# Third routed layer: the experts of the first six batches chosen inside the third attention, those of the last two behind it

## The chip, the cores and the metric

The kernel runs on one core of a Trainium2 chip. The metric is the device time of one execution in microseconds; the median of three runs before the change is 1176.97 us (1175.15 to 1178.13). A core has five engines with queues of their own: TensorE (PE, matmuls), VectorE (DVE), ScalarE (ACT), GpSimd (POOL) and SyncE (SP, which issues most DMAs). Each works through its instructions in order and waits on semaphores.

## The reference

Eight batches of 128 tokens with 256 features go through four layers. Each layer adds a gated cross-attention to `x` and then a gated feed-forward part. The change is in layer 2 (the third), whose feed-forward part chooses two of 16 experts for each token:

```
affinity = sigmoid(x @ centroids.T)                    # per token, 16 values
_, top_idx = top_k(affinity + gate_bias, 2)            # lower index first among equals
top_aff = take_along_axis(affinity, top_idx)
weights = top_aff / (top_aff.sum(-1) + 1e-9)
out = 0.1 * swiglu(x, shared) + sum over the two of weights[k] * swiglu(x, expert[top_idx[k]])
```

Here `x` stands for the normalised tokens behind the layer's attention (16 heads, one unit for each batch).

## The kernel before

`plan()` writes one list of steps; each engine's program goes through that list and emits its part of every step. So the order of the list is the order of each engine's queue. Inside an attention the list is put together by `merge`, which sorts thunks by a key: a stream has a start and an end, and its thunks are spread evenly between. The keys are in units (one unit of the third attention is one batch), with offsets from `TIMES[2]` (L148): `body` 1.604, `span` 1.053, `start` 0.084, `end` 3.227.

For unit `u` of the third attention the body (`st`, `pv`, `onorm`, seven thunks) is spread from u+1.604 to u+2.657. In it `st` makes scores on PE that DVE clips (L2008) and ACT exponentiates (L1716); `pv` multiplies them with the values; `oev` copies the result (ACT, L1730); `onorm` transposes it (PE, L1460) and divides by the sum (DVE, L2019 and L2022), one for each of four groups of heads. Then come `ot` and `oy` (transposes L1469, output projection L1258, DVE L2040 to L2045) and `oz` with `stats` (second normalisation and statistics of `x`, DVE L2055 to L2058 and L1877 to L1879, POOL L2409 and L2356). Behind each unit the finished batch is normalised (`fn`, DVE L1812), stored for the gathers (`tokens`, SP L1092), transposed (`xt`, L1266) and multiplied with the centroids (`xl`, PE L1258, copied to `lg` at L2063), at keys between u+3.327 and u+4.127. So the logits of batch 5 are there while unit 7 is in its body.

Behind the attention `sorted_pairs()` (L622) begins with a barrier on the last statistics. Then: `iota`; the shared expert's first two products `gu(0, 0)` and `gu(0, 1)` on PE (L1624, 16 matmul records); `route`, in which DVE chooses both experts of all eight batches (L2159 to L2186) with one exponential on ACT (L1744), and releases PE's count matmuls (L1501 to L1505) through `route_pe`; silu (ACT, L1797) and product (`gated2`, DVE, L2296) of the first half; `gu(1, 0)` and `gu(1, 1)`; `rank2`, in which DVE turns the counts into slots (from L2189); `invert` (PE L1611, DVE L2305 to L2311), which gives the token list; the loads of sorted tokens by POOL (L2429); `down2` (PE L1635, DVE L2321); then 31 tiles of sorted tokens (`tx`, `tu`, `th`, `td`), between which SP loads the keys of the next attention (`k3load`). Each of DVE's instructions in `route` and `rank2` waits for the one before it (`link`).

`first_max` (L1851) is the search for the first largest of the scores, five instructions; `route` uses it twice. The buffers `ra`, `rb`, `rc`, `oh` and `cm` lie in the third slot of `Pt`, where the attention's exponentials also go (columns 0 to 511 of each slot in this attention).

Of the kernel before, what the change touches and what calls it, by code (L numbers as in the profile page):

```python
# [72 lines left out]
P = 128  # L73
NB = 8
# [10 lines left out]
LOADS = 14  # L85
FFN1 = (11.35, 13.3, -0.95, 1.5, -0.9, 1.4)
FIRST_GROUP = 6
KEY_SPACE = 4
QUANT_PIECES = 5
SLOTW = 6144  # L90
# [62 lines left out]
def plan():  # L153
# [6 lines left out]
    def take(ring):  # L160
        ring = "B" if ring in "MS" else ring
        n[ring] += 1
        if ring == "B":
            s_count[(n["B"] - 1) % BANKS] = (n["B"] - 1) // BANKS + 1
        return n[ring] - 1

    def add(kind, **k):
        s = Record(kind=kind, **k)
        steps.append(s)
        return s  # L170
# [83 lines left out]
    def attention(A, later, before):  # L254
# [196 lines left out]
        for u in range(A.U):  # L451
            first, store, packs = front(u)
            if "fronts" in at:
                times = at["rest"] if u and "rest" in at else at["fronts"]
                assert len(times) == len(first)
                streams += [([thunk], u + t, u + t) for thunk, t in zip(first, times)]
            else:
                streams += [(first, u, u + at["front"])]
            streams += [(store, u + at["store"], u + at["store"]),
                        (packs, u + at["packs"], u + at["packs"] + 0.02)]  # L460
            if A.layer == 0:
                streams += [([lambda r=units[u]: add("bias", un=r)], u + at["body"], u + at["body"])]
            if A.layer == 0 and u == 0:
                at_group = FIRST_GROUP - 1 + at["end"]
                streams += [([lambda: choose0(0)], at_group + 0.95, at_group + 0.95),
                            ([lambda: rank0(0)], at_group + 1.3, at_group + 1.3),
                            ([lambda b=b: add("scatter", b=b) for b in range(FIRST_GROUP)], at_group + 1.45, at_group + 1.6)]
                streams += [([lambda: add("prepare", m=take("M"))], at["front"], at["front"]),
                            ([lambda: add("bias_out", m=take("M"))], at["max_first"], at["max_first"]),
                            ([lambda i=i: add("loads", i=i) for i in range(LOADS)], 2.0, 9.5)]  # L470
            if A.layer == 3 and u == 1:
                streams += [([lambda: add("w12load", s=last["td"])], u + at["body"] + 0.5, u + at["body"] + 0.5)]
            if A.has_max:
                begin = u + at["max"] if u else at["max_first"]
                step = (u + at["max_end"] - begin) / A.parts
                for tiles, split, turn in maxes(units[u]):
                    begin += step
                    streams += [(tiles, begin - step, begin), ([split], begin, begin),
                                ([turn], begin + at["neg"] - at["max_end"], begin + at["neg"] - at["max_end"])]
            body_end = u + at["body"] + at["span"]  # L480
            batches = range(units[u].b0, units[u].b0 + A.nb)
            streams += [(body(units[u]), u + at["body"], body_end), (finish(units[u]), body_end + at["start"], u + at["end"]),
                        ([f for b in batches for f in later(b)], u + at["end"] + 0.1, u + at["end"] + 0.9)]
# [26 lines left out]

    def group0(g):
        return (0, FIRST_GROUP) if g == 0 else (FIRST_GROUP, NB)

    def choose0(g):
        add("choose0", lm=last["lm"], exp_i=take("exp"), j=g, k=group0(g))
# [106 lines left out]
    def sorted_pairs():  # L622
# [5 lines left out]
        add("iota", m=take("M"))  # L628
        for ch in range(2):
            gate_up2(0, ch)()  # L630
        m_route = take("M")
        route(2, m_route)
        for tg in range(2):
            for ch in range(2):
                if tg:
# [115 lines left out]
def flamingo(nc, t, out):  # L751
# [13 lines left out]
    with ExitStack() as ctx:  # L765
# [53 lines left out]
        def expert(e, word, n):  # L819
# [59 lines left out]

        ra, rb, rc, oh, cm = [Pt[:, 2, 128 * i:128 * (i + 1)].rearrange("p (b e) -> p b e", b=NB)
                              for i in range(5)]
        ra0, rc0, oh0 = [tmp2[:, 64 * i:64 * (i + 1)].rearrange("p (b e) -> p b e", b=NB) for i in range(3)]
        sg = Pt[:, 0:2, 0:512]
        xe = qf[:, :, 0:256]
# [361 lines left out]
        def _(pe):  # L1248
# [36 lines left out]
            for s in steps:  # L1285
# [204 lines left out]
                elif s.kind == "rank0":  # L1490
# [4 lines left out]
                    pe.matmul(dst, lhsT=const("before"), rhs=oh0[:, b0:b1, :], start=True, stop=False)  # L1495
                    pe.matmul(dst, lhsT=const("ones"), rhs=rc0[:, b0:b1, :], start=False, stop=True
                              ).then_inc(bank_ready[s.m % BANKS], 1)
                elif s.kind == "route" and s.layer == 2:
                    dst = m_begin(s.m)
                    pe.wait_ge(route_pe, 1)  # L1500
                    pe.matmul(dst[:, 0:128], lhsT=const("before"), rhs=cm[:, :, :], start=True, stop=False)  # L1501
# [139 lines left out]
        def _(act):  # L1641
# [4 lines left out]
            for s in steps:  # L1646
# [90 lines left out]
                elif s.kind == "choose0":  # L1737
                    b0, b1 = s.k
                    act.wait_ge(route_a, s.exp_i + 1)
                    act.activation(ra0[:, b0:b1, :], ra0[:, b0:b1, :], ACT.Exp).then_inc(route_b, 1)  # L1740
                elif s.kind == "route":
                    act.wait_ge(route_a, s.exp_i + 1)
                    n = {2: 16, 3: 4}[s.layer]
                    act.activation(ra[:, :, 0:n], ra[:, :, 0:n], ACT.Exp, scale=-1.0 if s.layer == 2 else 1.0  # L1744
                                   ).then_inc(route_b, 1)
                elif s.kind == "ext":
                    e = s.i
                    turn(act, bank_ready, s.m)
# [52 lines left out]
        def _(dve):  # L1801
# [46 lines left out]
                link(dve.tensor_reduce(tmp2[:, 0:n // 4], tmp[:, 0:n].rearrange("p (w t) -> p w t", t=4), AX.X, ALU.add))  # L1848
                link(dve.tensor_copy(te[:, 0:n // 4], tmp2[:, 0:n // 4]))

            def first_max(src, E, onehot):  # L1851

                link(dve.tensor_reduce(r8[:, 0, :], src, AX.X, ALU.max))
                mx = r8[:, 0, :].unsqueeze(2).to_broadcast([P, NB, E])
                link(dve.tensor_tensor(rb[:, :, 0:E], src, mx, ALU.is_equal))
                desc = const("desc")[:, 0:E].unsqueeze(1).to_broadcast([P, NB, E])
                link(dve.tensor_tensor(rb[:, :, 0:E], rb[:, :, 0:E], desc, ALU.mult))
                link(dve.tensor_reduce(r8[:, 1, :], rb[:, :, 0:E], AX.X, ALU.max))
                m2 = r8[:, 1, :].unsqueeze(2).to_broadcast([P, NB, E])
                link(dve.tensor_tensor(onehot, rb[:, :, 0:E], m2, ALU.is_equal))  # L1860

            dve.memset(arena[:, 0:2048], 0.0)
            dve.memset(arena[:, 6144:8192], 0.0).then_inc(zeroed[0], 1)
# [4 lines left out]
            for s in steps:  # L1868
# [241 lines left out]
                    link(dve.tensor_tensor(gate, gate, keep, ALU.mult))  # L2110
                elif s.kind == "route":
                    evacuated(dve, s.lm)
                    n = {2: 16, 3: 4}[s.layer]
                    L = lg[:, :, 0:n]
                    if s.layer == 3:
                        link(dve.tensor_tensor(L, L, row("br3").unsqueeze(1).to_broadcast([P, NB, n]), ALU.add))
                    if s.layer == 3:
                        first_max(L, n, oh[:, :, 0:n])
                        mx = r8[:, 0, :].unsqueeze(2).to_broadcast([P, NB, n])
                        dve.tensor_tensor(ra[:, :, 0:n], L, mx, ALU.subtract).then_inc(route_a, 1)  # L2120
                        dve.wait_ge(route_b, s.exp_i + 1)
# [4 lines left out]
                    if s.layer == 3:  # L2126
# [27 lines left out]
                        link(dve.tensor_scalar(r8[:, 5, :], r8[:, 5, :], float(P), None, ALU.mult))  # L2154
                        link(dve.tensor_tensor(r8[:, 5, :], r8[:, 5, :], r8[:, 4, :], ALU.add))
                        dve.tensor_copy(idx[:, 0, :], r8[:, 5, :]).then_inc(routed3, 1)
                    else:

                        link(dve.tensor_scalar(ra[:, :, :], L, -87.0, None, ALU.max))  # L2159
                        dve.sem_inc(route_a, 1)  # L2160
                        dve.wait_ge(route_b, s.exp_i + 1)
                        link(dve.tensor_scalar(rc[:, :, :], ra[:, :, :], 1.0, None, ALU.add))
                        link(dve.reciprocal(ra[:, :, :], rc[:, :, :]))
                        gb = row("gb2").unsqueeze(1).to_broadcast([P, NB, 16])
                        link(dve.tensor_tensor(rc[:, :, :], ra[:, :, :], gb, ALU.add))
                        first_max(rc[:, :, :], 16, oh[:, :, :])
                        link(dve.tensor_scalar(lg[:, :, :], oh[:, :, :], -1e30, None, ALU.mult))
                        link(dve.tensor_tensor(rc[:, :, :], rc[:, :, :], lg[:, :, :], ALU.add))
                        first_max(rc[:, :, :], 16, lg[:, :, :])

                        for k, pick in enumerate((oh, lg)):
                            link(dve.tensor_tensor(cm[:, :, :], pick[:, :, :], ra[:, :, :], ALU.mult))
                            link(dve.tensor_reduce(wts[:, k, :], cm[:, :, :], AX.X, ALU.add))
                        link(dve.tensor_tensor(r8[:, 2, :], wts[:, 0, :], wts[:, 1, :], ALU.add))
                        link(dve.tensor_scalar(r8[:, 2, :], r8[:, 2, :], 1e-9, None, ALU.add))
                        link(dve.reciprocal(r8[:, 3, :], r8[:, 2, :]))
                        link(dve.tensor_scalar(r8[:, 3, :], r8[:, 3, :], tg[:, 6:7], None, ALU.mult))
                        link(dve.tensor_tensor(wts[:, :, :], wts[:, :, :], r8[:, 3, :].unsqueeze(1).to_broadcast([P, 2, NB]),
                                               ALU.mult))

                        link(dve.tensor_tensor(cm[:, :, :], oh[:, :, :], lg[:, :, :], ALU.add))
                        link(dve.memset(rc[:, 0, :], 0.0))
                        for b in range(1, NB):
                            link(dve.tensor_tensor(rc[:, b, :], rc[:, b - 1, :], cm[:, b - 1, :], ALU.add))
                        link(dve.tensor_tensor(ra[:, 0, :], rc[:, NB - 1, :], cm[:, NB - 1, :], ALU.add))
                        dve.sem_inc(route_pe, 1)  # L2186
                elif s.kind == "rank2":
# [367 lines left out]
```

## Time and profile before

| | us |
|---|---|
| median of three runs | 1176.97 |
| their range | 1175.15 to 1178.13 |
| the profiled execution | 1181.53 |
| its span, first to last instruction | 1179.7 |
| PE busy | 946.2 |
| DVE busy | 666.4 |
| ACT busy | 437.7 |
| POOL busy | 396.5 |

Busy time is the sum over all stages. An engine that is busy 80% of the span need not set its end: what counts at a place is which wait there ends last. The chain of waits follows the instruction that ended last back to what released it, step by step. A row of a timeline that says `[2.02 <-DVEq L2186]` tells that the engine sat idle for 2.02 us and that DVE's queue at line 2186 released it. The granted clock (PEclk) is a share of TensorE's full speed of 2.4 GHz.

### The profile page before, as it was taken

The numbers are of one execution on the slowest core, as the hardware profiler recorded it, in microseconds if no ns is written. First come the engines' busy times: TensorE is split into PE (matmuls) and PEld (weight loads), VectorE is DVE, ScalarE is ACT, GpSimd is POOL, SyncE is SP. The second block draws the span as 40 slices with busy tenths as digits, with TensorE's granted clock in tenths as the row PEclk, the third lists the DMA queues.
The fourth block names the chain that finished last, engine by engine and source line by source line (L and its number), as shares of the span: only waits on it lengthen the run. The fifth ranks groups of instructions, "written<-read, shape, count | busy, mean of one in ns | idle before, by whom it ended". The sixth has DMA issues, their size and how long they took to land.

```text
span 1179.7 us, 18929 instructions
## 1 busy us (share of the span) xinstructions
PE 946.2 (80%) x6638; PEld 557.1 (47%) x6638; DVE 666.4 (56%) x1588; ACT 437.7 (37%) x722; POOL 396.5 (34%) x530
## 2 busy tenths in 40 slices
PE   3899995789189999787699627999989997199992
PEld 1455544678044455565367412344434444156652
DVE  5778753452679433687663258788887852211111
ACT  1356662111046412444114200566556575022120
POOL 5232304332622003343034261356555565200002
PEclk9999997989579999898699956799999999599997
DMA  6434424684633003744318630101210002700002
GB/s 183 123 94 156 154 104 179 195 256 160 152 99 103 1 1 73 221 97 94 152 54 233 151 102 5 38 2 42 109 42 3 2 2 108 269 20 23 14 14 80
DMA packets 110107, 115.27 MB, mean 98 GB/s; under 512 B 58696, under 2 KB 99336, under 8 KB 106984
## 3 DMA queue, kind: packets, MB, share of 16 engines
q1 hardware_dynamic: 102912, 97.67, 26.9%
q0 software_dynamic: 3792, 10.36, 3.6%
q10 hardware_dynamic: 3312, 6.03, 1.4%
q8 instruction: 56, 0.92, 0.3%
q14 instruction: 35, 0.29, 0.1%
HBM read 88.17 MB, written 29.62 MB: 100 GB/s over the span
## 4 chain that ended last, share of the span: by engine, by line
PE 47%; DVE 15%; DMA 8%; issue 6%; POOL 4%; ACT 2%; SPq 1%; POOLq 0%; ACTq 0%; DVEq 0%
PE psT L1558 7%; PE psT L1258 6%; PE psT L1409 5%; PE psB L1373 4%; PE psB L1258 4%; DVE mxp L1972 4%; PE psO L1453 4%; PE psB L1572 3%; PE psB L1635 2%; DMA xn<-scr_tokens,token 2%; PE psO L1443 2%; PE psT L1521 2%; PE psO L1441 1%; PE psB L1599 1%; DMA scr_k_high<-sk 1%
## 5 line engine op out<-in xcount | busy, mean ns | idle before, releaser
L1972 DVE TENSOR_REDUCE mxp<-psB 128x1 f32<-128x512 f32 x256 | 163.7, 683 | 37.6 <-PE psB L1373 36.8
L1409 PE MATMUL psT<-whole 99*128 99x256 bf16 (+2 forms) x1024 | 153.3, 275 | 10.8 <-issue 10.0
L1976 DVE TENSOR_REDUCE mxp<-psB 128x2 f32<-128x512 f32 x192 | 123.4, 683 | 32.1 <-PE psB L1379 31.8
L1722 ACT ACTIVATE Pt<-psT,ln 128x1024 f32<-128x1024 f32 x96 | 106.5, 1113 | 64.6 <-PE psT L1409 63.5
L1409 PEld LDWEIGHTS psT<-whole 99*128 99x128 bf16 (+2 forms) x1024 | 96.6, 102 | 55.1 <-issue 22.9
L1722 ACT ACTIVATE Pt<-psT 128x1024 f32<-128x1024 f32 x96 | 97.9, 1023 | 57.6 <-PE psT L1409 56.1
L1373 PE MATMUL psB<-whole 96*128 96x512 bf16 x256 | 96.3, 427 | 24.6 <-DMA whole<-scr_q 14.0
L2356 POOL TENSOR_TENSOR rstd<-vare,cst 128x1 f32<-128x1 f32 x64 | 35.8, 562 | 231.0 <-DVE vare L1879 230.7
L1379 PE MATMUL psB<-whole 96*128 96x256 bf16 x384 | 78.2, 306 | 37.8 <-DMA whole<-scr_q 20.9
L1558 PE MATMUL psT<-whole,qf 128*128 x176 | 80.7, 602 | 0.6 <-ACT qf L1770 0.6
L2415 POOL TENSOR_SCALAR nb_t<-Pt 128x1024 f16<-128x1024 f32 x64 | 67.2, 1050 | 40.1 <-ACT Pt L1722 38.0
L1379 PEld LDWEIGHTS psB<-whole 96*128 96x128 bf16 x384 | 30.4, 104 | 86.3 <-issue 36.3
L2268 DVE TENSOR_TENSOR Pt<-psT,Pt 128x512 f32<-128x512 f32 x22 | 15.2, 691 | 98.7 <-ACT Pt L1776 98.7
L1441 PE MATMUL psO<-Pt,whole 128*32 128x256 f32 x768 | 63.2, 402 | 3.9 <-ACT Pt L1722 3.0
L1373 PEld LDWEIGHTS psB<-whole 96*128 96x128 bf16 x256 | 20.6, 100 | 89.0 <-issue 39.5
L1258 PE MATMUL psT<-xn_t,whole 128*128 128x512 f32 (+1 forms) x128 | 61.4, 631 | 0.0
L1453 PE MATMUL psO<-Pt,cst 128*32 128x256 f32 x768 | 59.0, 384 | 0.0
L2449 POOL DMA_INDIRECT xn_t<-scr_sorted_out,idx x8 | 7.6, 953 | 138.9 <-DMA scr_sorted_out<-xn 136.7
L1266 PE MATMUL psB<-cst,xn 128*128 128x128 f32 x96 | 22.9, 326 | 32.5 <-DVE xn L1812 31.7
L1460 PE MATMUL psB<-cst,Oe 128*128 128x128 f32 x160 | 37.6, 303 | 13.5 <-ACT Oe L1730 8.4
L1558 PEld LDWEIGHTS psT<-whole,qf 128*128 128x128 f32 x176 | 32.4, 194 | 33.4 <-issue 33.4
L2429 POOL DMA_INDIRECT xn<-scr_tokens,token x31 | 29.4, 949 | 53.8 <-DVE token L2311 28.6
(340 smaller groups left out, 1758.4 us busy)
## 6 DMA issues: line engine op xcount, KB each, us to landing
whole<-in_w SPq DMA_DIRECT2D x32, 512.0 KB, 5.3
whole<-in_w SPq DMA_DIRECT2D x5, 3072.0 KB, 10.7
scr_q<-sq SPq DMA_DIRECT2D x48, 96.0 KB, 2.1
whole<-scr_q SPq DMA_DIRECT2D x24, 192.0 KB
whole<-scr_k SPq DMA_DIRECT2D x24, 192.0 KB, 5.5
scr_sorted_out<-xn SPq DMA_DIRECT2D x31, 128.0 KB, 4.4
scr_k<-sk SPq DMA_DIRECT2D x32, 96.0 KB, 1.9
whole<-scr_k SPq DMA_DIRECT2D x24, 128.0 KB, 5.6
```

The source lines that it names most:

```text
L1258: ins = pe.matmul(dst, lhsT=lhs(kd), rhs=rhs(kd), start=(kd == 0), stop=(kd == halves - 1))
L1373: ins = pe.matmul(dst, lhsT=q_at[:, h * A.T + s.tc * P:h * A.T + (s.tc + 1) * P], rhs=k_at[:, h * NT + half * 512:h * NT + (half + 1) * 51 ...
L1379: ins = pe.matmul(dst[:, i * 256:(i + 1) * 256], lhsT=q_at[:, h * A.T + s.tc * P:h * A.T + (s.tc + 1) * P], rhs=k_at[:, h * A.T:(h + 1) * ...
L1409: ins = pe.matmul(psT[:, s.n % 2, i * A.T:(i + 1) * A.T], lhsT=k_at[:, h * kw + s.c * P:h * kw + (s.c + 1) * P], rhs=q_at[:, h * A.T:(h + ...
L1441: ins = pe.matmul(dst, lhsT=VA[:, u.g % 3, s.c * A.H + h, :], rhs=pr, start=first, stop=last)
L1453: ins = pe.matmul(dst, lhsT=const("sumsel"), rhs=pr, start=False, stop=last)
L1460: ins = pe.transpose(dst[:, tc * P:(tc + 1) * P], Oe[:, s.o % 2, tc * P:(tc + 1) * P], ident)
L1558: ins = pe.matmul(psT[:, s.n % 2, k * 512:(k + 1) * 512], lhsT=xeT[:, s.i % 2, kd, :], rhs=whole[:, bass.ds(s.un.k * SLOTW + at, 512)], st ...
L1722: act.activation(p_slot(A, s.p)[:, 0:4 * A.T], psT[:, s.n % 2, 0:4 * A.T], ACT.Exp, bias=bias, scale=scale).then_inc(T_used[s.n % 2], 1)
L1972: dve.tensor_reduce(mxp[:, s.un.g % 2, at:at + 1], psB[:, s.n % BANKS, :], AX.X, ALU.max).then_inc(bank_used[s.n % BANKS], 1)
L1976: dve.tensor_reduce(mxp[:, s.un.g % 2, at:at + 2], psB[:, s.n % BANKS, :].rearrange("p (h n) -> p h n", h=2), AX.X, ALU.max).then_inc(bank ...
L2415: pool.tensor_scalar(n_slot(s.p)[:, 0:w], p_slot(s.A, s.p)[:, 0:w], 1.0, OFFSET, ALU.mult, ALU.add).then_inc(rounded, 1)
```

## The change

The routing of layer 2 is cut into two groups of batches, 0 to 5 and 6 to 7. Each group has two steps: `scores2` (bound the logits on DVE, exponential on ACT) and `choose2` (all the rest of the choice on DVE, on the group's columns alone). The running count over the batches carries on from the first group to the second, whose `choose2` makes the total and releases the counts, a step of its own (`counts2`) with the same matmuls. The first group's steps are put into the third attention with the keys `at_group + 0.95` and `at_group + 1.2`, where `at_group` is 5 + 3.227; the second group's stand where `route` stood. The buffers move to columns 512 to 1023 of the third slot of `Pt`, and `cm` to the second slot, so that the attention's exponentials don't meet them. Layer 3 keeps `route`, with the same instructions.

```diff
+CHOOSE2_AT = 1.2
+SECOND_GROUP = 6
...
+            if A.layer == 2 and u == 0:
+                at_group = SECOND_GROUP - 1 + at["end"]
+                streams += [([lambda: scores2(0)], at_group + 0.95, at_group + 0.95),
+                            ([lambda: choose2(0)], at_group + CHOOSE2_AT, at_group + CHOOSE2_AT)]
...
+    def group2(g):
+        return (0, SECOND_GROUP) if g == 0 else (SECOND_GROUP, NB)
+
+    def scores2(g):
+        last["exp2"] = add("scores2", lm=last["lm"], exp_i=take("exp"), k=group2(g)).exp_i
+
+    def choose2(g):
+        add("choose2", exp_i=last["exp2"], k=group2(g))
...
             gate_up2(0, ch)()
-        m_route = take("M")
-        route(2, m_route)
+        scores2(1)
+        choose2(1)
+        m_route = add("counts2", m=take("M")).m
...
-        ra, rb, rc, oh, cm = [Pt[:, 2, 128 * i:128 * (i + 1)].rearrange("p (b e) -> p b e", b=NB)
-                              for i in range(5)]
+        ra, rb, rc, oh = [Pt[:, 2, 512 + 128 * i:640 + 128 * i].rearrange("p (b e) -> p b e", b=NB) for i in range(4)]
+        cm = Pt[:, 1, 768:896].rearrange("p (b e) -> p b e", b=NB)
...
-                elif s.kind == "route" and s.layer == 2:
+                elif s.kind == "counts2":
...
+                elif s.kind == "scores2":
+                    b0, b1 = s.k
+                    act.wait_ge(route_a, s.exp_i + 1)
+                    act.activation(ra[:, b0:b1, :], ra[:, b0:b1, :], ACT.Exp, scale=-1.0).then_inc(route_b, 1)
...
-            def first_max(src, E, onehot):
...
+            def first_max(src, E, onehot, b0, b1):
+                def wide(ap):
+                    return ap.unsqueeze(2).to_broadcast([P, b1 - b0, E])
+                work = rb[:, b0:b1, 0:E]
+                link(dve.tensor_reduce(r8[:, 0, b0:b1], src, AX.X, ALU.max))
+                link(dve.tensor_tensor(work, src, wide(r8[:, 0, b0:b1]), ALU.is_equal))
+                desc = const("desc")[:, 0:E].unsqueeze(1).to_broadcast([P, b1 - b0, E])
+                link(dve.tensor_tensor(work, work, desc, ALU.mult))
+                link(dve.tensor_reduce(r8[:, 1, b0:b1], work, AX.X, ALU.max))
+                link(dve.tensor_tensor(onehot, work, wide(r8[:, 1, b0:b1]), ALU.is_equal))
...
+                elif s.kind == "scores2":
+                    evacuated(dve, s.lm)
+                    b0, b1 = s.k
+                    dve.tensor_scalar(ra[:, b0:b1, :], lg[:, b0:b1, :], -87.0, None, ALU.max).then_inc(route_a, 1)
+                elif s.kind == "choose2":
+                    b0, b1 = s.k
+                    score, biased, first, second, both = [t[:, b0:b1, :] for t in (ra, rc, oh, lg, cm)]
+                    total, scale = r8[:, 2, b0:b1], r8[:, 3, b0:b1]
+                    dve.wait_ge(route_b, s.exp_i + 1)
+                    link(dve.tensor_scalar(biased, score, 1.0, None, ALU.add))
+                    link(dve.reciprocal(score, biased))
+                    gb = row("gb2").unsqueeze(1).to_broadcast([P, b1 - b0, 16])
+                    link(dve.tensor_tensor(biased, score, gb, ALU.add))
+                    first_max(biased, 16, first, b0, b1)
+                    link(dve.tensor_scalar(second, first, -1e30, None, ALU.mult))
+                    link(dve.tensor_tensor(biased, biased, second, ALU.add))
+                    first_max(biased, 16, second, b0, b1)
+
+                    for k, pick in enumerate((first, second)):
+                        link(dve.tensor_tensor(both, pick, score, ALU.mult))
+                        link(dve.tensor_reduce(wts[:, k, b0:b1], both, AX.X, ALU.add))
+                    link(dve.tensor_tensor(total, wts[:, 0, b0:b1], wts[:, 1, b0:b1], ALU.add))
+                    link(dve.tensor_scalar(total, total, 1e-9, None, ALU.add))
+                    link(dve.reciprocal(scale, total))
+                    link(dve.tensor_scalar(scale, scale, tg[:, 6:7], None, ALU.mult))
+                    link(dve.tensor_tensor(wts[:, :, b0:b1], wts[:, :, b0:b1],
+                                           scale.unsqueeze(1).to_broadcast([P, 2, b1 - b0]), ALU.mult))
+
+                    link(dve.tensor_tensor(both, first, second, ALU.add))
+                    if b0 == 0:
                         link(dve.memset(rc[:, 0, :], 0.0))
-                        for b in range(1, NB):
-                            link(dve.tensor_tensor(rc[:, b, :], rc[:, b - 1, :], cm[:, b - 1, :], ALU.add))
+                    for b in range(max(b0, 1), b1):
+                        link(dve.tensor_tensor(rc[:, b, :], rc[:, b - 1, :], cm[:, b - 1, :], ALU.add))
+                    if b1 == NB:
                         link(dve.tensor_tensor(ra[:, 0, :], rc[:, NB - 1, :], cm[:, NB - 1, :], ALU.add))
                         dve.sem_inc(route_pe, 1)
...
```

## Rows read from the trace of the kernel before

**Rows 1.** The page's head: the span of the profiled execution.
```profile
span 1179.7 us, 18929 instructions
```

**Rows 2.** Chain of waits, three stretches: start us, us, what was waited for.
```profile
565.91 0.66 PE psB L1266 x2
...
567.56 2.06 PE psB L1258 x4
569.64 0.43 DVE y_t L2040
...
579.39 0.24 DVE Pt L2159
...
620.39 8.03 DMA xn<-scr_tokens,token
...
1036.82 3.44 PE psT L1558 x8
```

**Rows 3.** Timeline of DVE, 560 to 570: start us, us, instruction, [idle before, releaser].
```profile
561.47 0.18 DVE L2019 RECIPROCAL rden<-psB 128x4 f32<-128x4 f32 x1 [0.21 <-DVE nb_t L2008]
...
564.67 0.22 DVE L2022 TENSOR_TENSOR On<-psB,rden 128x64 f32<-128x64 f32 x1
565.00 0.18 DVE L2019 RECIPROCAL rden<-psB 128x4 f32<-128x4 f32 x1
...
565.89 0.23 DVE L2022 TENSOR_TENSOR On<-psB,rden 128x64 f32<-128x64 f32 x1
569.64 0.42 DVE L2040 TENSOR_TENSOR y_t<-psB,rows 128x256 f32<-128x256 f32 x1 [3.53 <-PE psB L1258]
```

**Rows 4.** The same timeline of DVE, 579 to 602.
```profile
579.39 0.23 DVE L2159 TENSOR_SCALAR Pt<-lg 128x128 f32<-128x128 f32 x1
580.12 0.23 DVE L2162 TENSOR_SCALAR Pt<-Pt 128x128 f32<-128x128 f32 x1 [0.49 <-ACT Pt L1744]
580.38 0.95 DVE L2163 RECIPROCAL Pt<-Pt 128x128 f32<-128x128 f32 x1
581.37 0.29 DVE L2165 TENSOR_TENSOR Pt<-Pt,rows 128x128 f32<-128x128 f32 x1
...
587.22 0.20 DVE L2176 RECIPROCAL r<-r 128x8 f32<-128x8 f32 x1
...
588.40 1.43 DVE L2184 TENSOR_TENSOR Pt<-Pt 128x16 f32<-128x16 f32 x7
...
591.39 0.28 DVE L2189 COPY Pt<-psB 128x128 f32<-128x128 f32 x1
...
601.53 0.19 DVE L1847 TENSOR_TENSOR tmp<-tmp,w_at 128x32 f32<-128x32 f32 x1
```

**Rows 5.** Timeline of PE, 578 to 610.
```profile
578.56 9.67 PE L1258 MATMUL psT<-xn_t,whole 128*128 128x512 f32 x16
590.24 0.46 PE L1501 MATMUL psB<-Pt,cst 128*128 128x128 f32 x2 [2.02 <-DVEq L2186]
...
591.11 8.59 PE L1258 MATMUL psT<-xn_t,whole 128*128 128x512 f32 x16
599.98 0.63 PE L1611 MATMUL psB<-whole 128*128 128x64 bf16 x16 [0.28 <-DVE whole L2225]
...
604.77 4.58 PE L1635 MATMUL psB<-whole 128*128 128x256 f32 x20 [0.67 <-DVE x L2321]
```

**Rows 6.** Timeline of ACT, the silu behind the second `gu`.
```profile
588.27 0.60 ACT L1797 ACTIVATE nb_t<-psT 128x512 f32<-128x512 f32 x1 [2.84 <-PE psT L1258]
```

**Rows 7.** Stretches of the span; columns PE, PEld, DVE, ACT, POOL busy, PEclk, DMA share, GB/s.
```profile
564.00:566.00 2.00, 0.46 (x2) 0.20 (x3) 1.73 (x10) 0.00 (x0) 0.55 (x1) 0.50 0.00 0
...
582.00:584.00 2.00, 2.00 (x4) 0.93 (x3) 1.78 (x7) 0.00 (x0) 0.00 (x0) 0.54 0.96 406
...
590.00:595.00 5.00, 4.76 (x12) 2.76 (x13) 4.48 (x15) 0.00 (x0) 0.00 (x0) 0.66 0.00 0
...
605.00:610.00 5.00, 4.79 (x24) 3.99 (x23) 2.92 (x7) 0.39 (x2) 2.99 (x4) 1.00 0.35 105
```

More of the change, by code:

```diff
@@ L1740, in _ @@
                     act.activation(ra0[:, b0:b1, :], ra0[:, b0:b1, :], ACT.Exp).then_inc(route_b, 1)
+                elif s.kind == "scores2":
+                    b0, b1 = s.k
+                    act.wait_ge(route_a, s.exp_i + 1)
+                    act.activation(ra[:, b0:b1, :], ra[:, b0:b1, :], ACT.Exp, scale=-1.0).then_inc(route_b, 1)
                 elif s.kind == "route":
                     act.wait_ge(route_a, s.exp_i + 1)
-                    n = {2: 16, 3: 4}[s.layer]
-                    act.activation(ra[:, :, 0:n], ra[:, :, 0:n], ACT.Exp, scale=-1.0 if s.layer == 2 else 1.0
-                                   ).then_inc(route_b, 1)
+                    act.activation(ra[:, :, 0:4], ra[:, :, 0:4], ACT.Exp).then_inc(route_b, 1)
                 elif s.kind == "ext":
@@ L1849, in pack_tiles @@
                 link(dve.tensor_copy(te[:, 0:n // 4], tmp2[:, 0:n // 4]))
-            def first_max(src, E, onehot):
[L1853 to L1860, printed above, removed]
+            def first_max(src, E, onehot, b0, b1):
[8 more added lines that the diff above has]
+                link(dve.tensor_tensor(onehot, work, wide(r8[:, 1, b0:b1]), ALU.is_equal))
             dve.memset(arena[:, 0:2048], 0.0)
@@ L2112, in _ @@
                     evacuated(dve, s.lm)
-                    n = {2: 16, 3: 4}[s.layer]
+                    n = 4
                     L = lg[:, :, 0:n]
@@ L2117, in _ @@
                     if s.layer == 3:
-                        first_max(L, n, oh[:, :, 0:n])
+                        first_max(L, n, oh[:, :, 0:n], 0, NB)
                         mx = r8[:, 0, :].unsqueeze(2).to_broadcast([P, NB, n])
@@ L2156, in _ @@
                         dve.tensor_copy(idx[:, 0, :], r8[:, 5, :]).then_inc(routed3, 1)
[L2157 to L2181, printed above, removed]
```

## The prediction

> **What bounds the kernel now.** I read four views, in this order. The page first: one execution of 1179.7 us span [rows 1], a serial mix of engines. Then the chain of waits around the change. It runs without a break through the last unit of the third attention and the head of the third routed layer: DVE's last normalisations and `xn`, PE's transpose and output projection, DVE's `y_t`, and so on to the routing block at 579.39 [rows 2]. Each link waits for the one before, so a microsecond put on DVE's queue in front of one of them is a microsecond of the kernel, unless it falls into one of DVE's idle gaps. So the third view is DVE's timeline. From 561.47 to 566.12 DVE goes from one instruction to the next (only the first row shows an idle time, 0.21 us before it); its first real gap, 3.53 us, comes after the last `onorm` of the attention and before `y_t` at 569.64 [rows 3]. The routing block then holds DVE from 579.39 and ends with the eighth addition of the running count near 590.04 (seven of them 588.40 to 589.83, one more 0.2 behind): 10.65 us [rows 4]. The fourth view is PE beside it: the two shared-expert steps `gu(0, 0)` and `gu(0, 1)` take it from 578.56 to 588.23, then it idles 2.02 us, until the routing block has released the count matmuls at 590.24 [rows 5]. So PE is only 2.0 us better than DVE here. Call T the start of the routing block: DVE releases the counts at T+10.65, PE could take them at T+8.84.
>
> **What the change does to the queues.** No step of PE changes place. On DVE one block becomes two. The place of the first follows from the planner's keys. Unit 7's `body` has seven thunks between 8.604 and 9.657, so its sixth, with `pv(3)` and `onorm(2)`, has the key 9.431; the block `choose2(0)` gets 5+3.227+1.2 = 9.427 and stands just in front of it. `scores2(0)` (9.177) stands behind `oz(6)` and its `stats`, before `onorm(1)`. On DVE that is: one instruction before 564.67, and the whole choice of six batches between the end of `onorm(1)` and 565.00 [rows 3]. Behind it wait `onorm(2)`, `fn(6)`, `onorm(3)`, all that follows from them on PE, ACT and POOL, and the token stores on SP's queue. The 3.53 us gap lies behind the block, not under it.
>
> **Cost of the first block (six batches, 96 columns instead of 128).** An instruction costs its duration and about 0.03 us to the next (580.12+0.23 to 580.38; 580.38+0.95 to 581.37). A fp32 one with a tensor operand takes 0.29 at 128 columns [rows 4], the 32-column one 0.19 (the row at 601.53 of [rows 4]), so 0.255 at 96, with the gap 0.29. There are 17 of these (the biased score, five and five in the two searches for a maximum, the masked copy, four for the weights, the sum of both picks): 4.9 us. Two `tensor_scalar` of 0.23 at most, 0.25 each: 0.5. The reciprocal: 0.95 at 128 columns, 0.20 at 8, so 0.75 at 96, with its gap 0.8. Five small ones, of which the reciprocal at 587.22 is one, at 0.23: 1.1. The memset 0.1. The running count goes from seven additions to five, at 1.43/7 = 0.20: 1.0. Sum 8.4, with a doubt of 0.2 either way. `scores2(0)` adds 0.2 before `onorm(1)`. The exponential between them is hidden: DVE to ACT and back took 580.12-579.39 = 0.73 [rows 4], 0.5 of it after DVE's own instruction, and `onorm(1)` fills just that (its two instructions stand from 564.46 to 565.00 in the same view; the second is in [rows 3]). ACT holds behind `scores2(0)` the last two copies of the attention's output, but what they feed stands behind the block on DVE anyway. I take **8.6 us**. Ends: 7.7 if ACT and PE work that used to trail DVE is then ready and closes small gaps (the idle 0.21 and a part of the 0.66 of transposes), 9.3 if the exponential is waited for in full. It cannot go under the 3.53 gap, since the gap begins only when PE has what stands behind the block; were it placed there, the price would be 8.6-3.5 = 5.1.
>
> **What the second block saves (two batches, 32 columns).** Seventeen at 0.22 = 3.75; two at 0.21 = 0.4; reciprocal 0.20 + (0.75/120)*24 = 0.35, with the gap 0.4; five small 1.1; two additions and the last one 0.6; the score step 0.65 (0.73 with a narrower pair). Sum 6.9, against 10.65: DVE releases the counts 3.7 us earlier. But PE isn't there yet: `gu(0, 1)` ends at T+8.84 as before. The work of DVE was what covered those matmuls; with it gone, they are late next. The counts can start at T+8.87 instead of T+10.85, 1.97 earlier. Then `rank2` needs DVE, which first has the second `gated2`: its silu starts at T+8.88 [rows 6], ends 0.60 later, the product takes 0.6, so `rank2` starts at about T+10.15 against 591.39-579.39 = 12.0 [rows 4]. Gain **1.85 us**. From there DVE runs `rank2` to the release of `invert` in the same time. PE's `gu(1, 0)` and `gu(1, 1)` took 8.59 beside it, ending 0.28 before `invert` [rows 5]; they start 1.9 earlier too. Everything behind (`invert`, the token list, POOL's loads, `down2`) moves as one piece. Bounds of the gain: 3.7 if PE is out of the way (eight records of this shape take 3.44 us at full clock [rows 2], so the 16 need 6.9 and end at T+6.1), and -2.1 if the clock stays at half throughout (13.8, ending at T+12.9).
>
> **The clock.** TensorE was granted half its clock (1.2 GHz) in the attention's tail, the stretch 564 to 566 standing for all two-us stretches from 560 to 582; it rose to full (2.4 GHz) at the end of 582 to 584, some 5 us into `gu(0, 0)` [rows 7]. Then, after the 2.02 us in which PE idled for the counts, the stretch 590 to 595 reads 0.66. In the changed kernel that first gap closes, so `gu(1, 0)` may run at full clock; DVE's `rank2` is then the bound and nothing is won, while a gap of about 2 us opens in front of `invert` instead. The earlier gap of this size was followed by half clock, but a third of the five us from 590 to 595 was at full again, so I take the slowed stretch behind the new gap to be over before DVE frees the bank for the fourth `down2` product: 20 records that then ran at full in 4.58 us [rows 5, 7]. At worst these run at half and cost 4.6 more. The Trainium skill (TensorE: Matmul & The Clock Gate, "HAM oscillation — how this bites in real kernels") says that idle stretches between bursts of matmuls put the clock back to half, and that each burst then starts slow. The trace agrees with it at 590. If the rule struck `down2` whole, the sum would be near +11; by the rows it is +6.75.
>
> **Sum.** 8.6 - 1.85 = +6.75 us on the profiled execution (1181.53 us, of which the span is 1179.7). That execution lies 4.6 above the median of the runs, 1176.97, and none of the stretches is one that varies; so 1176.97+6.75 = **1183.7 us**, 0.57% slower. Below 0.3% (3.5 us) a measurement of this kernel, whose three runs spread over 3 us, can't tell a change from none.
>
> **Rivals.**
> (a) DVE alone bounds the head of the layer: the clock rises early enough that `gu(0, 1)` is done before the second block. Gain 3.7: +4.9, 1181.9. For it: the rise came 5 us into PE's work and may come earlier. Against: a whole 2 us must be found.
> (b) The clock goes the other way: late in `gu(0, 0)` (+2.1 in place of -1.85), or half through `down2` (+4.6). +10.7 or +11.4, taken as 1187.7. For it: the row at 0.66 after a gap of the same size. Against: DVE covers the first part of `down2`.
> (c) The first block falls into PE's wait after all (a late `onorm` on DVE costs nothing because the transposes were not ready): 5.1-1.85 = +3.3, 1180.2, within the bound. Against: no idle before 566.12 on DVE.
> (d) Not slower: the 31 tiles behind the routing wait three times about 8 us (the first 8.03 [rows 2]) for an indirect load of tokens, while the key loads for the next attention share the DMA engines. If the new phase between PE, POOL and SP lets one of these loads land ahead of the key load, a wait goes: 6.75-8.0 = -1.3, 1175.7; two of them, 1168. It decides from a load that is issued one key load earlier. Against: both streams are released by the same tile steps and move together.
>
> **Chances.** Forecast 0.60, (a) 0.10, (b) 0.12, (c) 0.09, (d) 0.09. Slower by over 0.3%: forecast, (a) and (b), 0.82. Within 0.3%: (c) and half of (d), 0.14. Faster: 0.04. The range from 1179.5 to 1188.5 holds the forecast with its 7.7 to 9.3 for the block, (a), (b) and (c), and leaves out (d).
>
> **What the changed profile would show.** Right: some 34 DVE instructions in one piece between `onorm(1)` and `onorm(2)` of the last unit, 8.4 us, in the chain of waits, with PE and ACT idle beside the end of it; then the same 3.53 us gap; from `scores2(1)` to the counts 8.9 us, with the count matmuls waiting for no engine and standing directly behind `gu(0, 1)`; the clock at full in `gu(1, 0)`. Wrong: the 3.53 gap shorter or gone (c), a DVE wait before the counts (a), `gu(0, 0)` at half through its end or `down2` over 8 us (b), fewer than three waits of about 8 us in the tiles (d). A time under 1180.5 would refute the forecast.

## The result, and the profile after

The changed kernel takes 1181.65 us (median of 20 runs, 1174.93 to 1184.97), the kernel before 1176.77 us on the same occasions (20 runs, 1171.67 to 1184.7). The ratio is 1.0035 with a 95% interval of 1.002 to 1.0051: +4.1 us (2.4 to 6.0), slower, as forecast. Timed differences here and below come from the ratio, applied to the time of the kernel before; the two medians alone differ by 4.9 us. The forecast was +6.75 us, which lies outside the interval.

The profiled execution has a span of 1178.3 us, 1.4 less than that of before, though the kernel is slower. So spans don't show where the time went; stretches do. DVE's timeline of the attention's last unit comes first (start, duration, instruction, and in brackets the idle time before it with its releaser):

```profile
560.28 0.20 DVE L2178 TENSOR_SCALAR Pt<-lg 128x96 f32<-128x96 f32 x1
560.39 0.17 DVE L2037 RECIPROCAL rden<-psB 128x4 f32<-128x4 f32 x1
560.60 0.22 DVE L2040 TENSOR_TENSOR On<-psB,rden 128x64 f32<-128x64 f32 x1
560.83 0.22 DVE L2184 TENSOR_SCALAR Pt<-Pt 128x96 f32<-128x96 f32 x1
561.08 0.75 DVE L2185 RECIPROCAL Pt<-Pt 128x96 f32<-128x96 f32 x1
561.87 0.26 DVE L2187 TENSOR_TENSOR Pt<-Pt,rows 128x96 f32<-128x96 f32 x1
...
568.30 1.01 DVE L2207 TENSOR_TENSOR Pt<-Pt 128x16 f32<-128x16 f32 x5
569.34 0.18 DVE L2037 RECIPROCAL rden<-psB 128x4 f32<-128x4 f32 x1
...
573.99 0.42 DVE L2058 TENSOR_TENSOR y_t<-psB,rows 128x256 f32<-128x256 f32 x1 [3.54 <-PE psB L1274]
```

The first block stands between `onorm(1)` and `onorm(2)`, from 560.83 to 569.34: 8.51 us without an idle time, and behind it the same gap as before, 3.54 in place of 3.53 [rows 3]. The second block, behind the barrier, in the same view:

```profile
583.74 0.18 DVE L2178 TENSOR_SCALAR Pt<-lg 128x32 f32<-128x32 f32 x1
584.28 0.18 DVE L2184 TENSOR_SCALAR Pt<-Pt 128x32 f32<-128x32 f32 x1 [0.35 <-ACT Pt L1760]
584.50 0.35 DVE L2185 RECIPROCAL Pt<-Pt 128x32 f32<-128x32 f32 x1
584.88 0.19 DVE L2187 TENSOR_TENSOR Pt<-Pt,rows 128x32 f32<-128x32 f32 x1
...
590.38 0.17 DVE L2209 TENSOR_TENSOR Pt<-Pt 128x16 f32<-128x16 f32 x1
590.70 0.69 DVE L2320 TENSOR_TENSOR whole<-psT,nb_t 128x512 f32<-128x512 f32 x1
592.04 0.69 DVE L2320 TENSOR_TENSOR whole<-psT,nb_t 128x512 f32<-128x512 f32 x1 [0.65 <-ACT nb_t L1815]
592.65 0.28 DVE L2213 COPY Pt<-psB 128x128 f32<-128x128 f32 x1
```

T is now 583.74. DVE releases the counts at T+6.8 (against T+10.65), then has to wait 0.65 us for the silu of `gu(0, 1)`, and `rank2` starts at T+8.91 in place of T+12.0 [rows 4]. PE's timeline beside it:

```profile
582.91 8.46 PE L1274 MATMUL psT<-xn_t,whole 128*128 128x512 f32 x16
591.21 0.38 PE L1517 MATMUL psB<-Pt,cst 128*128 128x128 f32 x2
...
591.80 7.11 PE L1274 MATMUL psT<-xn_t,whole 128*128 128x512 f32 x16
601.24 0.63 PE L1627 MATMUL psB<-whole 128*128 128x64 bf16 x16 [2.33 <-DVE whole L2249]
```

The count matmuls follow `gu(0, 1)` with no idle time where 2.02 us stood before [rows 5]; `gu(1, 0)` and `gu(1, 1)` take 7.11 in place of 8.59; a gap of 2.33 us has opened before `invert`. The clock (sixth value behind the stretch's length: PE, PEld, DVE, ACT, POOL busy, PEclk, DMA share, GB/s):

```profile
582.00:584.00 2.00, 2.00 (x7) 1.48 (x7) 0.80 (x4) 0.00 (x0) 0.00 (x0) 0.50 0.59 221
584.00:586.00 2.00, 2.00 (x3) 0.78 (x3) 1.48 (x7) 1.51 (x2) 0.00 (x0) 0.55 0.94 406
586.00:588.00 2.00, 2.00 (x6) 0.95 (x5) 1.70 (x9) 0.02 (x1) 0.00 (x0) 1.00 1.16 487
...
600.00:605.00 5.00, 3.21 (x28) 2.59 (x28) 4.51 (x15) 0.00 (x0) 0.00 (x0) 1.00 0.00 0
```

It rose some 3 us into `gu(0, 0)`, in the profile of before 5 us into it [rows 7], and it stayed at full through the new gap.

All the stretches side by side, each read from DVE's timeline of its own profile (us). A: `y_t` of unit 6 to `y_t` of unit 7. B: on to T, the first routing instruction behind the barrier. C: T to the first instruction of `rank2`. D: on to the first tile's output copy. E: to the last tile's. F: to the first combine. "gu" is the time of the 16 records of `gu(0, 0)` and `gu(0, 1)` on PE. The last column is the timed ratio to the kernel before.

| kernel | A | B | C | D | E | F | sum | gu | ratio (95%) |
|---|---|---|---|---|---|---|---|---|---|
| before | 10.75 | 9.75 | 12.00 | 23.39 | 55.99 | 7.67 | 119.55 | 9.67 | |
| changed | 19.27 | 9.75 | 8.91 | 23.75 | 55.25 | 6.99 | 123.92 | 8.46 | 1.0035 (1.002 to 1.0051) |
| f0, changed again | 19.28 | 9.75 | 9.33 | 23.77 | 55.52 | 6.93 | 124.58 | 8.88 | 1.0046 (1.0021 to 1.007) |
| e1, block behind `onorm(3)` | 16.36 | 9.74 | 9.17 | 23.38 | 56.01 | 6.89 | 121.55 | 8.72 | 0.9993 (0.9975 to 1.0012) |
| e2, block alone | 19.25 | 9.76 | 11.93 | 23.38 | 56.28 | 7.02 | 127.62 | 8.65 | 1.0043 (1.0016 to 1.0069) |
| e3, both behind | 10.75 | 9.75 | 17.54 | 23.39 | 55.95 | 6.97 | 124.35 | 8.86 | 1.0021 (0.9998 to 1.0043) |
| e4, changed, PE kept busy | 18.18 | 8.78 | 8.17 | 23.76 | 56.32 | 7.00 | 122.21 | 7.03 | 1.0019 (0.9997 to 1.004) |
| f1, weights in the tiles | 10.75 | 9.75 | 9.96 | 23.41 | 58.09 | 7.54 | 119.50 | 9.52 | 0.9982 (0.996 to 1.0004) |
| f2, pieces in gaps | 11.53 | 9.75 | 9.59 | 23.40 | 58.90 | 6.98 | 120.15 | 9.14 | 1.0004 (0.9984 to 1.0024) |
| f3, f2 and PE busy | 11.53 | 9.58 | 6.74 | 23.43 | 58.89 | 7.00 | 117.17 | 7.03 | 0.9986 (0.9965 to 1.0007) |
| h1, f3, weights last | 11.52 | 9.58 | 6.74 | 23.39 | 55.53 | 6.95 | 113.71 | 7.03 | 0.9959 (0.9937 to 0.9981) |
| h2, f1, weights last | 10.75 | 9.75 | 9.57 | 23.39 | 56.46 | 7.00 | 116.92 | 8.25 | 0.9973 (0.9956 to 0.9991) |
| h3, before, PE busy | 10.76 | 8.79 | 12.07 | 23.45 | 56.55 | 7.69 | 119.31 | 7.03 | 0.9991 (0.9975 to 1.0007) |

For the changed kernel: A +8.52, C -3.09, D +0.36, E -0.74, F -0.68, sum +4.37, beside a measured +4.1.

### The profile page after: what moved, and what is told of

Same layout as the page of the kernel before. It is cut to its first block, busy times and chain, and to the rows that moved or that the text cites. A ratio compares the mean times of both kernels' runs of the same rounds, so it can differ in the third digit from the quotient of the medians.

```text
span 1178.3 us, 18955 instructions
## 1 busy us (share of the span) xinstructions
PE 940.2 (80%) x6638; PEld 554.3 (47%) x6638; DVE 670.2 (57%) x1614; ACT 437.4 (37%) x723; POOL 397.2 (34%) x530
## 4 chain that ended last, share of the span: by engine, by line
PE 47%; DVE 14%; DMA 8%; issue 7%; POOL 5%; ACT 2%; SPq 1%; POOLq 0%; ACTq 0%; DVEq 0%
PE psT L1574 7%; PE psT L1274 6%; PE psT L1425 5%; PE psB L1389 4%; DVE mxp L1990 4%; PE psB L1274 4%; PE psO L1469 3%; PE psB L1588 3%; PE psB L1651 2%; PE psO L1459 2%; PE psT L1537 1%; DMA scr_k_high<-sk 1%; PE psO L1457 1%; DMA xn<-scr_tokens,token 1%; PE psB L1615 1%
## 5 line engine op out<-in xcount | busy, mean ns | idle before, releaser
L1738 ACT ACTIVATE Pt<-psT 128x1024 f32<-128x1024 f32 x96 | 97.9, 1023 | 59.0 <-PE psT L1425 57.4
L1274 PE MATMUL psT<-xn_t,whole 128*128 128x512 f32 (+1 forms) x128 | 58.8, 608 | 0.0
```

The source lines that it names most:

```text
L1274: ins = pe.matmul(dst, lhsT=lhs(kd), rhs=rhs(kd), start=(kd == 0), stop=(kd == halves - 1))
L1738: act.activation(p_slot(A, s.p)[:, 0:4 * A.T], psT[:, s.n % 2, 0:4 * A.T], ACT.Exp, bias=bias, scale=scale).then_inc(T_used[s.n % 2], 1)
```

## The experiments

One per cent of this kernel is 11.8 us, and the intervals above reach some 2 to 3 us to either side, so the sizes are read from one profile of each kernel. The timed interval holds the sum of the stretches for eleven of the twelve (in e2 only just); for e1 it doesn't, as said there.

**e1: the first block behind the last `onorm`.**

```diff
-CHOOSE2_AT = 1.2
+CHOOSE2_AT = 1.4
```

> The changed kernel with the first block's key 9.627 in place of 9.427, so that it stands behind the last onorm of the third attention and in front of xt(6). Theory (the block costs its whole length where it stands, less the DVE gap that it falls into): 8.5 - 3.5 = 5.0 for the block, gain behind the barrier 1.9 to 3.1 as before, so 3.5 us faster than the changed kernel and +0.5 to +3 us on the kernel before (0.1 to 0.25% slower), with y_t of the last unit 5.0 us later than the gap would have let it. Rival (the place does not matter, since the block is hidden in part wherever it stands): as the changed kernel, +4 us.

Measured: -0.8 us against before (-3.0 to +1.4), and its interval does not touch that of the changed kernel: the place decides, the rival falls. The size is less sure. The expected +0.5 to +3 us overlaps the interval only in part, and the sum of the stretches, +2.0 us, lies 0.6 above its upper end; why is open. In the profile, DVE:

```profile
558.61 0.18 DVE L2037 RECIPROCAL rden<-psB 128x4 f32<-128x4 f32 x1 [0.70 <-PE psB L1476]
...
567.12 1.01 DVE L2207 TENSOR_TENSOR Pt<-Pt 128x16 f32<-128x16 f32 x5
568.17 0.42 DVE L2058 TENSOR_TENSOR y_t<-psB,rows 128x256 f32<-128x256 f32 x1
```

The 3.54 us gap before `y_t` is gone, so A grew by 5.6 against before, in place of 8.5. This is 0.6 more than the expected 5.0: a new wait of 0.70 us stands before `onorm(2)`. ACT holds the last two output copies behind the exponential of `scores2(0)`, which waits for DVE, so PE's transposes come late. In the changed kernel the block covers this wait.

**e2: the block alone.** The second group chooses all eight again; in the first one the second pick goes to a spare buffer, so that the logits stay.

```diff
-        return (0, SECOND_GROUP) if g == 0 else (SECOND_GROUP, NB)
+        return (0, SECOND_GROUP) if g == 0 else (0, NB)
...
+        spare = Pt[:, 0, 768:896].rearrange("p (b e) -> p b e", b=NB)
...
-                    score, biased, first, second, both = [t[:, b0:b1, :] for t in (ra, rc, oh, lg, cm)]
+                    score, biased, first, second, both = [t[:, b0:b1, :] for t in (ra, rc, oh, lg if b1 == NB else spare, cm)]
```

> The first six batches are chosen in the attention as in the changed kernel, and the second block chooses all eight again, so that the block in the attention is added and nothing is taken away behind the barrier. Theory: +8.6 us on the kernel before (0.73%), DVE from the release of the scores to the release of the counts 10.7 us as before, PE waiting for the counts. Rival (the block is half hidden and the gain is small, 5 - 1): +5 us. What this kernel has over the changed one is the gain of the second block: 1.85 by the prediction, 3.1 by the changed kernel's profile.

The profile shows A +8.50 and C 11.93, the full price and no gain, and the sum +8.1. The timed difference, +5.1 us (1.9 to 8.1), is the rival's number; it holds the profile's sum only at its end and not the expected +8.6. For the theory speaks the one profile, in which the block stands at full price and the other stretches moved by 0.4 us together; the time and the profile differ by 3 us here, and no further run settles it. What PE does is worth a look:

```profile
583.45 8.65 PE L1275 MATMUL psT<-xn_t,whole 128*128 128x512 f32 x16
595.07 0.46 PE L1518 MATMUL psB<-Pt,cst 128*128 128x128 f32 x2 [2.96 <-DVEq L2211]
...
595.85 7.11 PE L1275 MATMUL psT<-xn_t,whole 128*128 128x512 f32 x16
```

With the routing unsplit behind the barrier a faster `gu` (8.65 against 9.67) only makes PE's wait longer. So, by the profiles, the gain of the second block is C of this kernel less C of the changed one: 3.0 us.

**e3: both groups behind the barrier.** `scores2(0)` and `choose2(0)` leave the attention and stand in front of `scores2(1)`.

> The choice is split as in the changed kernel, but both groups stand behind the barrier. DVE then needs some 0.7 + 8.5 + 6.9 = 16 us from the first score step to the counts, in place of 10.7. Theory (only DVE's order counts): +5.3 us (0.45%), and PE idle before the counts for 7 us in place of 2. Rival (the clock adds to it): the longer idle time of PE puts the clock to half, gu(1, 0) and gu(1, 1) take up to 13.8 us beside the 8.4 us of rank2 and invert comes late: +8 to +10 us.

C grew by 5.5 us, the sum by 4.8; timed, +2.5 us (-0.2 to +5.1). The time decides against the rival's +8 to +10. The split itself costs this much: 8.5 and 6.8 us in two parts where 10.65 did in one. The clock did fall in PE's long wait (the stretch 588 to 590 reads 0.50), and the rival's price did not come:

```profile
590.87 0.77 PE L1518 MATMUL psB<-Pt,cst 128*128 128x128 f32 x2 [8.04 <-DVEq L2211]
...
592.14 8.38 PE L1275 MATMUL psT<-xn_t,whole 128*128 128x512 f32 x16
600.93 0.63 PE L1628 MATMUL psB<-whole 128*128 128x64 bf16 x16 [0.41 <-DVE whole L2250]
```

A part of the 16 records at half clock makes them 8.4 us, no longer than `rank2` beside them.

**e4: the changed kernel with PE kept busy.** The step `busy` stands in PE's queue under the block (12 matmuls, key `at_group + 1.4`) and in the gap before the last batch (9, `at_group + 1.8`).

```diff
+                elif s.kind == "busy":
+                    for _ in range(s.k):
+                        pe.matmul(psO[:, 0, :], lhsT=ident, rhs=cst[:, 0:256], start=True, stop=True)
```

> The changed kernel with 12 and 9 spare matmuls (128x256 f32 into a psum bank that this attention does not use) in PE's queue, under the first block and in the gap before the last batch's transposes. Theory: the clock is at full before the barrier, so gu(0, 0) and gu(0, 1) take 6.9 us in place of 8.5, the second block is the bound (gain 3.7 in place of 3.1), and the output projection of the last unit takes 1.0 in place of 2.0 us: 2 to 3.5 us faster than the changed kernel, +1 to +2 us on the kernel before. Rival (the clock does not rise under these, or it gives nothing because DVE bounds the tail): as the changed kernel, or slower by up to 2 us where the spare matmuls end late.

```profile
581.32 7.03 PE L1276 MATMUL psT<-xn_t,whole 128*128 128x512 f32 x16
589.12 0.46 PE L1522 MATMUL psB<-Pt,cst 128*128 128x128 f32 x2 [0.77 <-DVEq L2215]
```

The clock was at full when `gu(0, 0)` began, and now PE waits 0.77 us for DVE: C is 8.17, bound by the second block and the two products behind it. A and B are 1.1 and 1.0 us shorter: the last projections run at full clock. A, B and C together won 2.8 us, as expected; but E is 1.1 us longer than in the changed kernel, so the sum is only 1.7 less, below the 2 to 3.5 expected. Timed, +2.2 us against before (-0.4 to +4.7). The clock of this kernel behind the second gap, the one before `invert` (here 1.85 us):

```profile
600.00:602.00 2.00, 2.00 (x6) 1.49 (x6) 1.61 (x10) 0.00 (x0) 0.00 (x0) 0.52 0.00 0
602.00:604.00 2.00, 2.00 (x7) 1.47 (x7) 2.00 (x6) 0.00 (x0) 1.05 (x1) 0.62 0.00 0
```

The granted clock was at half for most of these stretches, and it cost nothing: `down2` begins and ends as far behind `invert` as in the changed kernel, and D is 23.76 beside 23.75 there.

**f0: the changed kernel again.**

> The changed kernel itself once more, on the same chip as the three below. If the block costs 8.5 us and the gain depends on when the clock rises in gu(0, 0), the profile again shows 8.5 us between onorm(1) and onorm(2), and the gain (12.0 less the time from the second score step to rank2) lies between 1.9 (rise as late as in the profile of before) and 3.9 (rise before the barrier; DVE then bounds). If the earlier rise belongs to the change, the gain is 3.1 again and the 16 records take 8.5 us.

+5.4 us (2.5 to 8.3). Block 8.5 again, C 9.33 with `gu` at 8.88: the gain lies inside the expected span and is not the same number. The early rise doesn't belong to the change: without the split `gu` took 8.25 (h2), 9.52 (f1) and 9.67 us (before), with it 8.46 to 9.14.

**f1 and f2: the weights off the path, the block in two pieces.** The weights of both picks (nine instructions) are needed only for the combine. f1 moves them, in a step of their own and with the scores in a buffer of their own, in the unsplit kernel; f2 in the split one, and cuts the first block at the second search.

```diff
-                        for k, pick in enumerate((oh, lg)):
-                            link(dve.tensor_tensor(cm[:, :, :], pick[:, :, :], ra[:, :, :], ALU.mult))
...
+            if t == 8:
+                add("weights2")
```

For f2 also `CHOOSE2_AT = 1.4`, and a step `second2` (second `first_max`, sum, running count) at `at_group + 2.4`, behind `fn(7)`, and behind `choose2(1)`.

> The kernel before, not split; only the nine DVE instructions that make the weights (585.52 to 587.93 in the profile of before, 2.4 us) are moved out of the routing block into the tile stage, where DVE is busy a third of the time and the weights are needed only behind it. The scores go to a buffer of their own. Theory (what the counts don't need has no business in front of them; DVE bounds the head of the layer by 2.0 to 3.1 us over PE): rank2 starts 2.4 us earlier, at T+9.6, and the kernel is 2.4 us (0.2%) faster. Rival (PE is the bound as soon as anything is taken off DVE): 1.9 us or less, where the clock rises as late as in the profile of before; and a tile step late by 2 us where the weights stand would give all of it back.

> The changed kernel with the weights moved as in f1 and the first block cut in two: scores, bias, the first search (10 instructions, 3.3 us) behind the last onorm, in the 3.54 us gap of DVE; the second search, the sum and the running count (2.9 us) behind fn(7), in its 2.42 us gap. Theory (a block costs its length less the gap it falls into): 0.1 + 0 + 0.5 us in the attention, and behind the barrier the bound of PE, 8.9 to 9.2 in place of 12.0: in all 2.2 to 2.5 us faster than the kernel before, 6 faster than the changed one. Rival (every DVE instruction before the barrier costs its time, gap or not): 6.3 - 3.1 = 3 us slower than before.

Both did their part in front: f1's C is 9.96, f2's 9.59 at 0.8 us more in A. And both lost it in the tiles, where E went from 56 to 58.1 and 58.9: the rival named for f1, for a step as cheap as 2.4 us. So neither reached what was expected (some 2.4 us faster): the sums are -0.05 and +0.6 us; timed, f1 -2.1 us (-4.7 to +0.5), f2 +0.5 us (-1.9 to +2.8). f2's DVE, and PE behind it:

```profile
627.29 0.42 DVE L2289 COPY xn<-psB 128x256 f32<-128x256 f32 x1 [1.62 <-DMA scr_sorted_out<-xn]
627.63 0.28 DVE L2213 TENSOR_TENSOR Pt<-Pt 128x128 f32<-128x128 f32 x1
...
630.02 0.17 DVE L2219 TENSOR_TENSOR w_at<-w_at,r 128x16 f32<-128x16 f32 x1
630.23 0.29 DVE L2281 TENSOR_TENSOR Pt<-psT,Pt 128x128 f32<-128x128 f32 x1
...
630.72 0.30 PE L1551 MATMUL psB<-cst,Pt 128*128 128x128 f32 x1 [1.08 <-DVEq L2284]
```

DVE is idle some 60% of that stage, but in short gaps (0.2 to 2.3 us) inside a loop over three engines, and PE is busy in 48.6 of the 55 us from 615 to 670. Behind the nine linked instructions PE waits 1.08 us for DVE's queue; in the kernel before, its longest wait for DVE's queue in the tiles is 0.37 us. That accounts for a part of the 2.1 and 2.9 us; the rest wasn't followed. That the weights' place makes the loss, h1 and h2 show.

**f3: f2 with spare matmuls** (one before `xt(6)`, seven at `at_group + 1.8`).

> f2 with spare matmuls (one before xt(6), seven in PE's gap of 5.7 us) in PE's queue. Theory (with the choice out of DVE's way the clock of the first gu steps is what is left): the clock rises before the barrier, the 16 records of gu(0, 0) and gu(0, 1) take 7 us, rank2 starts at T+7.0 in place of T+9, xt(7) and xl(7) take 0.7 us less: 2 to 2.7 us faster than f2, 4.5 to 5 us (0.4%) faster than the kernel before. Rival (the clock does not rise for so short a stretch): as f2, or 0.5 us slower from the last spare matmul.

C is 6.74, 2.85 less than in f2, at an equal A; the tiles still cost 3 us. So f3 is 3.0 us faster than f2 by the sums, and only 2.4 faster than the kernel before, not 4.5 to 5. Timed, -1.7 us (-4.1 to +0.8).

**h1, h2, h3.** h1 is f3, h2 is f1, each with the weights moved behind the last tile; h3 is the kernel before with f3's spare matmuls alone.

```diff
-            if t == 8:
-                add("weights2")
...
         last["td"] = tiles[TILES2 - 1].s
+        add("weights2")
```

> f3 with the weights behind the last tile, in front of the first combine, where DVE waits 6.3 us for the gathers (f3's profile); in the tile stage they had made it 58.9 us long in place of 55.3 to 56.3. Theory (they fit that gap): the tile stage is back at 56 us, the stretch from the last tile to the combine stays 7.0, and the kernel is 2.7 us faster than f3 and 4.7 us (0.4%) faster than the kernel before: +0.8 in the attention, -0.2 before the barrier, -5.3 up to rank2. Rival (the long tile stage comes from something else in the split, such as the earlier start of the token loads): 58.9 us again, and 2 us faster than before at most.

> f1 (the kernel before, not split) with the weights in front of the first combine. Theory: 2.0 to 2.4 us off the head of the layer and the tile stage back at 56 us: 2.0 to 2.4 us (0.2%) faster than the kernel before. Rival: as f1, which lost 2.1 us in the tiles.

> The kernel before with f3's spare matmuls alone. Theory (DVE bounds the head of the layer in the kernel before, whatever the clock): the 16 records of gu(0, 0) and gu(0, 1) take 7.0 us in place of 8.5 to 9.7, rank2 still starts 12.0 us behind the first routing instruction, and nothing but 0.2 us in the last transposes is won. Rival (the clock is worth its microseconds in either kernel): 2 us faster.

h1's DVE:

```profile
664.24 0.28 DVE L2217 TENSOR_TENSOR Pt<-Pt 128x128 f32<-128x128 f32 x1
...
666.43 0.17 DVE L2223 TENSOR_TENSOR w_at<-w_at,r 128x16 f32<-128x16 f32 x1
...
670.85 0.48 DVE L2299 SCALAR_TENSOR_TENSOR x<-whole,w_at,x 128x256 f32<-128x256 f32 x1 [3.86 <-DMA ctx_t<-scr_sorted_out,idx]
```

The weights stand in the wait for the gathers, which still has 3.86 us left; E is 55.5 again. h1 beats both kernels: -4.8 us against before (-7.4 to -2.2), its stretches -5.8. h2, without the split and without spare matmuls, gets -3.2 us (-5.2 to -1.1), its stretches -2.6. h3 shows what the clock is worth where DVE bounds:

```profile
575.79 7.03 PE L1260 MATMUL psT<-xn_t,whole 128*128 128x512 f32 x16
587.42 0.52 PE L1506 MATMUL psB<-Pt,cst 128*128 128x128 f32 x2 [4.60 <-DVEq L2191]
```

`gu` takes 7.03 and PE waits 4.60 us in place of 2.02; C is 12.07. It won 1.0 us in B, more than the 0.2 expected: the last transposes and logits run at full clock here, while in f3 the block's second piece stands on DVE in just that gap and hides them. E is 0.6 us longer, so the sum is only 0.2 under that of before. Timed, -1.1 us (-2.9 to +0.8), which holds the rival's 2 us too; against the rival speaks C.

## Why the prediction was right, and which term was mis-sized

- **The place of the first block.** Right to the instruction: between `onorm(1)` and `onorm(2)`, with the 3.53 us gap behind it and not under it. e1 shows the gap's worth.
- **Its price.** 8.6 us forecast, 8.4 of them for the block and 0.2 for the score step. The block took 8.51 and A grew by 8.52, so the score step cost next to nothing.
- **PE takes over as the bound behind the barrier.** Right: the counts follow `gu(0, 1)` without idle time, and DVE waits for the silu. They came at T+7.5, though, in place of T+8.9.
- **The gain, 1.85 us.** This term was mis-sized: 3.09 in the profile, 2.67 in f0's. Its arithmetic holds. In the five kernels where PE bounds C (changed, f0, e1, f1, f2) it is the duration of the 16 `gu` records plus 0.45, and the 9.67 of before plus 0.45 is 10.12, the forecast's T+10.15. What failed is taking 9.67 from one execution, with the words that none of the stretches is one that varies: nine profiles without spare matmuls have 8.25 to 9.67, and the one of before is the slowest. The two `gu` steps are the same work; what differs is when the clock rises in them. The forecast had this mechanism as rival (a), whose full 3.7 needs the clock up before the barrier, as e4 has it (3.8). Rival (a) itself didn't come: DVE has no wait before the counts, PE is still the bound. By the time alone one couldn't tell: (a) at +4.9 and (c) at +3.3 both lie nearer to +4.1 than the forecast. The profile tells, with the gap whole (not c) and PE as the bound (not a).
- **The clock behind the new gap (rival b).** The gap opened as forecast (2.33 us), the clock stayed at 1.00 to 605 and `down2` cost nothing. The rule of the Trainium skill quoted there (TensorE: Matmul & The Clock Gate, "HAM oscillation — how this bites in real kernels"), that idle stretches between bursts put the clock back to half, did not strike at this gap. In e3, with 8.04 us before the counts, the clock did fall, and there the trace agrees with it. It also fell in e4, behind 1.85 us before `invert`. Neither fall cost time: D is 23.39 in e3, as before, and 23.76 in e4, as in the changed kernel.
- **The tiles (rival d).** Its price came from a misreading. The "waits of about 8 us" are trips of single loads in the chain, from issue to landing (8.03, 7.27 and 7.80 us), and not idle time: from 615 to 670 PE is busy 49.55 of the 55 us and its longest idle time is 1.30 us. So an earlier landing had some 1.3 us to win there, not 8. In the changed kernel's chain stand two such loads (7.11 and 7.34 us) and one store (6.67), and E is just 0.7 shorter. E and F came out 1.4 us shorter than in the profile of before and D 0.4 longer, which the forecast left at nothing. For E this is scatter: the ten kernels without the weights in the tiles have 55.25 to 56.55. Why D is 23.8 in changed, f0 and e4 and 23.4 elsewhere is open. F is 0.7 us: the last store landed in 1.68 us in place of 2.35. F is 7.5 to 7.7 in before, f1 and h3 and 6.9 to 7.0 elsewhere, h2 among them; why is open.

With a gain of 2.9 for 1.85 the sum would have been +5.7; the rest down to the measured 4.1 lies within its interval.

## What to carry to other kernels

Splitting a serial block to run a part of it earlier pays only by the idle time that the early part really falls into. Find the gap on that engine in the timeline and check on which side of it the queue puts the block: here 0.2 of a key cost 3 us. Before splitting, take out of the block what the release at its end doesn't need, and put it where the engine waits for something long; an engine idle most of a tight loop is not such a place. And a duration that holds a clock rise is a sample: read it in several executions before it becomes a bound.

## What the runs showed of the hardware

The same 16 matmul records behind the same barrier took 8.25 to 9.67 us, and 7.03 when PE had been kept busy before. Whether a gap puts the clock down was not set by its length alone: the 16 records behind an idle time of 2.02 us took 8.59 (before), behind 2.96 us 7.11 (e2), behind 4.60 us 8.43 (h3) and behind 8.04 us 8.38 (e3). Before `invert`, the clock stayed at 1.00 behind 2.33 us (changed) and fell behind 1.85 us (0.52 in the stretch from 600 to 602, e4).

In front of the changed stretch the executions differ more than the change is worth: `y_t` of unit 6 came at 551.8 us (e1) to 558.9 us (before), with the same instructions in front of it.
